# Column sums in 32-column tiles, and low parts made on Pool, in a gated attention-and-feed-forward block

## The chip, the cores and the metric

The kernel runs on one core of a Trainium2 chip. The metric is the device time of one execution in microseconds. Before the change it is 604.24 us, the median of three runs (603.97 to 604.48).

## What is computed

For each of two sequences of 1,024 rows of x (2,048 columns, f32) and a context of 2,048 x 2,048 the reference computes

```python
def fake_quant(x, scale, zp):
    q = clip(round(x / s + z), 0, 255)
    return (q - z) * s
x = x + tanh(g_xattn[0]) * (fake_quant(layernorm(x)) @ fake_quant(ctx))
x = x + tanh(g_ffn[0]) * (layernorm(x) @ (U * S @ V.T).T)      # rank 512
```

## The kernel before

The 2,048 rows are 16 tiles of 128 (NT = 16, eight to a context, TB = 8). Three stages follow each other for each tile on TensorE: `s1(t)` multiplies the quantised, transposed x by the quantised context (4 column quarters of 512, 16 matmuls each, 64 in all); `mm3(u)` multiplies the second normalised x, split into an f16 high and low part, by V, split likewise into v_hl (per half g of 8 k-tiles: 16 matmuls with V's high part, then 8 with its low part); `mm4(u)` multiplies that result by U (12 matmuls for each quarter). TensorE's list stands in full at L670 to L745.

Quantised values are held centred (q minus a rounded zero point, in bf16). What the fraction of the zero point takes away is added back as a correction: a row sum (`bvec`, from ScalarE's accumulator) and a column sum of the context (`corr`, L850). The column sums of the first context are matmuls by a 128 x 128 matrix of ones, one per k-tile (L516, 64 in all). Those of the second context already go in 32-column tiles (L520): four k-tiles each write 32 partitions of the bank, and two further f16 matmuls add the four groups up (L529, L530).

The first context is loaded in 32 chunks of 2 k-tiles x 512 columns (512 KB each), block n of 8 chunks being quarter n of the columns. For each chunk one engine makes u8 of f32 (ScalarE L756; Pool for chunks 1 to 5; DVE L1127 for the chunks of WHOLE, 27 and 31), and Pool (L252, even chunks) or DVE (L1131, odd ones) makes bf16. TensorE takes each chunk at once: two column sums, then two matmuls for each of tiles 0, 1 and 2 (in block 3 for tile 0 alone; tiles 1 and 2 follow whole, then tile 3's `s1`). Tiles 0 to 2 are transposed by TensorE, tile 3 by a DMA (L330).

For each tile and quarter Pool adds the row correction (L258, once a tile) and `corr` (L263) to x in `ring`, and DVE adds the product from PSUM (L1137) and takes its statistics (L1139): `x1_unit(t, n)`. When tile u has all four, DVE and ScalarE work out scale and bias. ScalarE writes x's high part (L811), DVE normalises into `xn` (L1174) and subtracts (L1177, `x_lo_half`), and SP issues the transposing DMA (L339). V arrives in 8 pieces of 2 k-tiles, is squared for a norm by ScalarE (L859), summed by TensorE (L668, `norm_sums`), scaled on ScalarE into its high part (L877) and on DVE into its low part (L1246, `v_low`, one instruction per piece). U's high and low parts (L884, L1252) follow `norm(1)`, which waits for `norm_sums(1)`.

Every engine's order is written out by hand: SP at L402 to L483 (all loads, stores and transposes in one queue), TensorE at L670, ScalarE at L887, DVE at L1255, Pool at L274. Each engine works its list in order and waits on semaphores of the others. Stages hold 10 chunks, so the load of chunk c waits until chunk c - 10 has been read. The pairs of loops at L693 and L1270 set the order in which chunks and tiles alternate.

## Time and profile before

| | |
|---|---|
| median of 3 runs | 604.24 us (603.97 to 604.48) |
| profiled execution | 604.71 us, span from first to last instruction 602.9 us |
| TensorE matmuls busy | 582.7 us (97%) |
| DVE, ScalarE, Pool busy | 381.7 us (63%), 212.4 us (35%), 191.4 us (32%) |
| granted TensorE clock | 1.00 over the whole span |
| moved by DMA | 102.21 MB, 387 GB/s in slices 2 to 4 of 40 (15 to 60 us) |

The duration of one matmul in the timeline includes its latency (0.38 us for 512 columns), so the start of the next is what tells its cost. Times of the timeline are from the span's first instruction. A row with xN joins N instructions in sequence, and a bracket at its end tells how long the engine stood before it and who released it.

### The profile page before, as it was taken

The numbers are of one execution on the slowest core, as the hardware profiler recorded it, in microseconds if no ns is written. First come the engines' busy times: TensorE is split into PE (matmuls) and PEld (weight loads), VectorE is DVE, ScalarE is ACT, GpSimd is POOL, SyncE is SP. The second block draws the span as 40 slices with busy tenths as digits, with TensorE's granted clock in tenths as the row PEclk, the third lists the DMA queues.
The fourth block names the chain that finished last, engine by engine and source line by source line (L and its number), as shares of the span: only waits on it lengthen the run. The fifth ranks groups of instructions, "written<-read, shape, count | busy, mean of one in ns | idle before, by whom it ended". The sixth has DMA issues, their size and how long they took to land.

```text
span 602.9 us, 7571 instructions
## 1 busy us (share of the span) xinstructions
PE 582.7 (97%) x2816; PEld 266.4 (44%) x2816; DVE 381.7 (63%) x703; ACT 212.4 (35%) x258; POOL 191.4 (32%) x149
## 2 busy tenths in 40 slices
PE   1899999999999999999999999999999999999998
PEld 1344444444444444445444444444444444444444
DVE  6939989995288962845375975647365665735212
ACT  5798978822041432456623310303011030301000
POOL 2899650002223419726505800220404030030000
DMA  8999985639828795998835344370906345181512
GB/s 280 387 387 387 309 240 128 116 122 196 239 55 240 186 216 189 241 304 268 241 123 150 81 84 54 66 190 12 223 35 147 116 90 172 30 163 20 138 53 104
DMA packets 143828, 102.21 MB, mean 170 GB/s; under 512 B 106672, under 2 KB 106928, under 8 KB 143792
## 3 DMA queue, kind: packets, MB, share of 16 engines
q1 hardware_dynamic: 134800, 84.43, 53.1%
q10 hardware_dynamic: 8992, 17.30, 9.2%
q8 instruction: 22, 0.36, 0.2%
q14 instruction: 14, 0.11, 0.1%
HBM read 58.99 MB, written 16.78 MB: 126 GB/s over the span
## 4 chain that ended last, share of the span: by engine, by line
PE 75%; DMA 11%; DVE 8%; issue 3%; SPq 2%; ACT 1%; POOL 1%; DVEq 0%; ACTq 0%
PE bank L553 23%; PE bank L584 16%; PE bank L651 8%; PE bank L650 8%; PE bank L655 8%; PE bank L589 8%; DMA v_hl<-in_ctx_dram 8%; DMA xT<-xs 4%; DVE v_hl L1246 1%; DVE xn L1174 1%; DVE xs L1177 1%; DVE ring L1137 1%; SPq L311 1%; PE bank L520 1%; POOL u8r L243 1%
## 5 line engine op out<-in xcount | busy, mean ns | idle before, releaser
L553 PE MATMUL bank<-q,qT 128*128 128x512 bf16 x896 | 201.5, 380 | 0.3 <-DVE ring L1137 0.3
L553 PEld LDWEIGHTS bank<-q,qT 128*128 128x128 bf16 x896 | 87.7, 98 | 107.1 <-issue 1.5
L258 POOL TENSOR_SCALAR ring<-ring,bvec 128x2048 f32<-128x2048 f32 x16 | 32.8, 2050 | 269.7 <-DVE bvec L1119 269.7
L584 PE MATMUL bank<-v_hl,xT 128*128 128x512 f16 x512 | 115.8, 379 | 0.9 <-DMA xT<-xs 0.9
L263 POOL TENSOR_TENSOR ring<-ring,corr 128x512 f32<-128x512 f32 x64 | 87.0, 1390 | 23.2 <-ACT corr L850 22.1
L651 PE MATMUL bank<-u_hl,hbuf 128*128 128x512 f16 x240 | 91.1, 380 | 0.0
L650 PE MATMUL bank<-u_hl,hbuf 128*128 128x512 f16 x240 | 91.0, 379 | 0.0
L1137 DVE SCALAR_TENSOR_TENSOR ring<-bank,const,ring 128x512 f32<-128x512 f32 x64 | 47.6, 743 | 58.2 <-PE bank L553 55.9
L1210 DVE SCALAR_TENSOR_TENSOR ring<-bank,cy,ring 128x512 f32<-128x512 f32 x63 | 46.4, 747 | 52.8 <-PE bank L655 52.8
L252 POOL TENSOR_SCALAR q<-u8r,const 128x1024 bf16<-128x1024 uint8 x52 | 63.9, 1236 | 45.4 <-ACT u8r L756 41.7
L584 PEld LDWEIGHTS bank<-v_hl,xT 128*128 128x128 f16 x512 | 49.8, 98 | 61.2 <-DMA xT<-xs 1.9
L797 ACT ACTIVATE ln<-ln,const 128x1 f32<-128x1 f32 x16 | 4.7, 294 | 189.8 <-DVE ln L1150 189.8
L655 PE MATMUL bank<-u_hl,hbuf 128*128 128x512 f16 x240 | 61.6, 379 | 0.0
L589 PE MATMUL bank<-v_hl,xT 128*128 128x512 f16 x256 | 60.6, 379 | 0.0
L1177 DVE TENSOR_TENSOR xs<-xn,xs 128x1024 f16<-128x1024 f32 x32 | 46.8, 1461 | 9.7 <-ACT xs L811 8.8
L1078 DVE BATCH_NORM_STATS2 st<-ring 128x6 f32<-128x512 f32 x64 | 40.3, 680 | 10.3 <-DMA ring<-in_x_dram 10.2
L1139 DVE BATCH_NORM_STATS2 st<-ring 128x6 f32<-128x512 f32 x64 | 44.5, 695 | 2.2
L811 ACT ACTIVATE xs<-ring,ln 128x1024 f16<-128x1024 f32 x32 | 38.2, 1233 | 20.4 <-DVE ln L1162 14.8
L589 PEld LDWEIGHTS bank<-v_hl,xT 128*128 128x128 f16 x256 | 25.0, 98 | 30.4 <-DVE v_hl L1246 0.4
L650 PEld LDWEIGHTS bank<-u_hl,hbuf 128*128 128x128 f16 x240 | 23.5, 98 | 28.5 <-issue 0.4
L655 PEld LDWEIGHTS bank<-u_hl,hbuf 128*128 128x128 f16 x240 | 23.5, 98 | 28.3
L1193 DVE SCALAR_TENSOR_TENSOR hbuf<-bank,hbuf 128x512 f16<-128x512 f32 x16 | 11.0, 687 | 39.4 <-ACT hbuf L825 39.4
(136 smaller groups left out, 493.3 us busy)
## 6 DMA issues: line engine op xcount, KB each, us to landing
out_dram<-ring SPq DMA_DIRECT2D x63, 256.0 KB, 3.5
ring<-in_x_dram SPq DMA_DIRECT2D x62, 256.0 KB, 3.9
v_hl<-in_ctx_dram SPq DMA_DIRECT2D x26, 512.0 KB, 11.5
stage<-in_ctx_dram ACTq DMA_DIRECT2D x17, 512.0 KB, 5.8
u_hl<-in_L_ffn_V_dram SPq DMA_DIRECT2D x8, 512.0 KB, 11.5
corr<-in_ctx_dram ACTq DMA_DIRECT2D x8, 512.0 KB, 6.7
stage<-in_ctx_dram SPq DMA_DIRECT2D x6, 512.0 KB, 11.5
q<-in_ctx_dram ACTq DMA_DIRECT2D x4, 512.0 KB, 8.8
```

The lines of the kernel that those rows point to most:

```text
L252: nc.gpsimd.tensor_scalar(q2_chunk(c), u8r[:, c % NU8, :], C_NC2, 1.0, ALU.add, ALU.mult)\
L263: nc.gpsimd.tensor_tensor(xq(t, n), xq(t, n), corr[:, n * W:(n + 1) * W], ALU.add).then_inc(x1_pre, 1)
L553: mm = nc.tensor.matmul(unit_bank(t, n)[:, :], qT_of(t)[:, k, :], q2[:, n, k, :], start=(k == 0), stop=(k == KT - 1))
L584: nc.tensor.matmul(h_bank(u)[:, :], xT[:, g, half, k % 8, :], v_hl[:, k, 0, :], start=(g == 0 and a == 0 and half == 0), stop=False)
L589: mm = nc.tensor.matmul(h_bank(u)[:, :], xT[:, g, 0, k % 8, :], v_hl[:, k, 1, :], start=False, stop=(g == 1 and a == 7))
L650: nc.tensor.matmul(y_bank(i)[:, :], t_hi[:, r, :], u_hl[:, n, r, 0, :], start=(r == 0), stop=False)
L651: nc.tensor.matmul(y_bank(i)[:, :], t_lo[:, r, :], u_hl[:, n, r, 0, :], start=False, stop=False)
L655: mm = nc.tensor.matmul(y_bank(i)[:, :], t_hi[:, r, :], u_hl[:, n, r, 1, :], start=False, stop=(r == RT - 1))
L1137: stt(xq(t, n), unit_bank(t, n)[:, :], C_A, xq(t, n), ALU.mult, ALU.add).then_inc(x1_ready, 1)
L1139: nc.vector.bn_stats(st2[:, t % R, n, :], xq(t, n)).then_inc(st2_ready, 1)
L1177: tt(xs[:, g, 1, :], xn[:, :], xs[:, g, 0, :], ALU.subtract).then_inc(xs_lo, 1)
L1210: stt(xq(u, n), y_bank(i)[:, :], cy[:, n:n + 1], xq(u, n), ALU.mult, ALU.add).then_inc(y_ready, 1)
```

## The change

- The first context's column sums go in the 32-column tiles of L520, in groups of two chunks (`colsum_pair`, behind every odd chunk). ScalarE copies the bank, divided by 32, to `corr` (`first_parts`), and one f32 matmul with ones adds the groups up (`first_total`). `column_correction(0, n)` waits for that.
- In block 3 TensorE takes tiles 0 and 1 (N3 = 2).
- WHOLE gains chunks 15, 19 and 23 (u8 made on DVE, not on ScalarE).
- SP loads all chunks first, then V's eight pieces (before, four of them alternated with the last four chunks).
- Tile 3's statistics, scale and u8 come one block sooner on DVE; ScalarE's and Pool's parts of it likewise (`op2(3)`, `pre_row(3)`).
- Pool makes V's low parts 3, 5 and 7, in two instructions each, and the normalised x of tiles 1, 2 and 3 (six halves). DVE still subtracts for x.
- `norm_sums(0)` moves into tile 3's `s1`, `norm_sums(1)` into mm3(1), behind its first high part.
- The lists of ScalarE and DVE are rewritten.

```diff
+    V_POOL = (3, 5, 7)
+    XN_POOL = (1, 2, 3)
+    N3 = 2
-        WHOLE = (27, 31)
+        WHOLE = (15, 19, 23, 27, 31)
...
+            def v_low(i):                                  # Pool
+                k = slice(2 * VORD[i], 2 * VORD[i] + 2)
+                pool.wait_ge(split_hi, i + 1)
+                nc.gpsimd.tensor_scalar(v_raw[:, k, :], v_raw[:, k, :], wsc[:, 3, 0:1], 1.0, ALU.mult, ALU.mult)\
+                    .then_inc(v_scaled, 1)
+                pool.wait_ge(v_scaled, V_POOL.index(i) + 1)
+                nc.gpsimd.tensor_tensor(v_hl[:, k, 1, :], v_raw[:, k, :], v_hl[:, k, 0, :], ALU.subtract)\
+                    .then_inc(v_lo_pool, 1)
+            def normalised_x(u, g):
+                pool.wait_ge(ln2_ready, u + 1)
+                pool.wait_ge(xs_lo, 2 * u + g)
+                nc.gpsimd.tensor_scalar(xn[:, :], xhalf(u, g), mean, scale, ALU.subtract, ALU.mult).then_inc(xn_pool, 1)
...
+            pre_row(G)
             for t in range(G):
                 pre(t, NQ - 1)
...
+                    if t == G:
+                        v_low(3)
+                        v_low(5)
+                        normalised_x(1, 0)
+                        v_low(7)
+                        normalised_x(1, 1)
+                        for u in XN_POOL[1:]:
+                            for g in range(2):
+                                normalised_x(u, g)
...
-            for c in range(12, CB - 4):
+            for c in range(12, CB):                        # SP
                 load_chunk(c)
-            for i in range(4):
-                load_v(VORD[i])
-                load_chunk(CB - 4 + i)
-            for i in range(4, CQ):
+            for i in range(CQ):
                 load_v(VORD[i])
...
+            def first_total(n):                            # TensorE
+                pe.wait_ge(parts_ready, n + 1)
+                nc.tensor.matmul(colsum_bank(0, n)[:, :], ones_f[:, :], corr[:, n * W:(n + 1) * W],
+                                 start=True, stop=True).then_inc(colsum_summed, 1)
+            def colsum_pair(n, i):
+                colsum(0, n, CK * (i - 1), CK * i + CK)
...
             for n in range(1, NQ):
                 for i in range(CQ):
-                    colsum(0, n, CK * i, CK * i + CK)
-                    for t in range(G if n < NQ - 1 else 1):
+                    need_chunk(CQ * n + i)
+                    if i % 2 == 1:
+                        colsum_pair(n, i)
+                    for t in range(G if n < NQ - 1 else N3):
                         s1_part(t, n, CK * i, CK * i + CK)
-            s1_part(1, NQ - 1)
-            s1_part(2, NQ - 1, 0, 12)
+                    if i == 1:
+                        first_total(n - 1)
+            for t in range(N3, G - 1):
+                s1_part(t, NQ - 1)
+            s1_part(2, NQ - 1, 0, 4)
+            first_total(NQ - 1)
+            s1_part(2, NQ - 1, 4)
+            s1_part(G, 0, 0, 8)
             norm_sums(0)
-            s1_part(2, NQ - 1, 12)
-            s1(G)
+            s1_part(G, 0, 8)
+            for n in range(1, NQ):
+                s1_part(G, n)
             mm3(0)
-            norm_sums(1)
             mm3(1)
...
+            def first_parts(n):                            # ScalarE
+                act.wait_ge(colsum_done, n + 1)
+                nc.scalar.activation(corr[:, n * W:(n + 1) * W], colsum_bank(0, n)[:, :], ACT.Copy,
+                                     scale=1.0 / GW).then_inc(parts_ready, 1)
...
+            first_parts(2)
+            op1(30)
             v_square(VORD[0])
+            v_square(VORD[1])
             column_correction(0, 2)
-            for j in VORD[2:6]:
+            for j in VORD[2:5]:
                 v_square(j)
+            first_parts(3)
+            v_square(VORD[5])
+            v_square(VORD[6])
             column_correction(0, 3)
-            for j in VORD[6:8]:
-                v_square(j)
+            v_square(VORD[7])
...
                     op2(c)                                 # DVE
-                    if n == 1 and i == 0:
+                    if n == 0 and i == 0:
                         sums1(3)
-                    elif n == 1 and i == 1:
                         variance1(3)
-                    elif n == 1 and i == 2:
+                    elif n == 0 and i == 1:
                         quantise(3)
...
             norm(0)
+            x_lo_half(0, 0)
             x1_unit(1, NQ - 1)
             x1_unit(2, NQ - 1)
-            x_lo_half(0, 0)
+            x1_unit(3, 0)
             x_lo_half(0, 1)
-            x1_unit(3, 0)
             v_low(0)
             variance2(1)
             v_low(1)
             scale2(1)
-            for i in range(2, 4):
-                v_low(i)
+            v_low(2)
             x_lo_half(1, 0)
-            for i in range(4, VP):
-                v_low(i)
+            v_low(4)
+            v_low(6)
             x_lo_half(1, 1)
             variance2(2)
+            hid_lo(0)
             norm_sum_up(1)
             scale2(2)
             norm(1)
-            hid_lo(0)
             u_low(0)
             x_lo_half(2, 0)
+            u_low(1)
             x_lo_half(2, 1)
-            u_low(1)
```

## Rows read from the trace of the kernel before

**Rows 1.** The page: busy time of each engine.
```profile
PE 582.7 (97%) x2816; PEld 266.4 (44%) x2816; DVE 381.7 (63%) x703; ACT 212.4 (35%) x258; POOL 191.4 (32%) x149
```

**Rows 2.** Waits of TensorE: us in total, times, longest.
```profile
PE bank L516 <- POOL q L252: 13.6, 4, 11.3
```

**Rows 3.** Timeline of TensorE: start us, us, engine, line, instruction, count.
```profile
49.12 0.60 PE L516 MATMUL bank<-q,ones_b 128*128 128x512 bf16 x2
...
62.93 0.60 PE L516 MATMUL bank<-q,ones_b 128*128 128x512 bf16 x2
...
77.95 13.98 PE L553 MATMUL bank<-q,qT 128*128 128x512 bf16 x64
91.77 3.62 PE L584 MATMUL bank<-v_hl,xT 128*128 128x512 f16 x16
...
108.12 3.63 PE L584 MATMUL bank<-v_hl,xT 128*128 128x512 f16 x16 [0.41 <-DMA xT<-xs]
```

**Rows 4.** Timeline of TensorE around column sums of the second context.
```profile
320.65 1.03 PE L655 MATMUL bank<-u_hl,hbuf 128*128 128x512 f16 x4
321.61 1.05 PE L520 MATMUL bank<-q,ones_b 128*32 128x512 bf16 x16
322.59 0.39 PE L553 MATMUL bank<-q,qT 128*128 128x512 bf16 x1
```

**Rows 5.** L668: durations ns (min/median/max) of f32; the page's group of bf16 loads.
```profile
L668 PEld LDWEIGHTS bank<-ssq,ones_f x4: 190/190/191, 76.7 to 102.2; 128*128 128x128 f32 x4
...
L553 PEld LDWEIGHTS bank<-q,qT 128*128 128x128 bf16 x896 | 87.7, 98 | 107.1 <-issue 1.5
```

**Rows 6.** Timeline of DVE and of Pool, 43 to 52 us.
```profile
44.56 0.75 DVE L1137 SCALAR_TENSOR_TENSOR ring<-bank,const,ring 128x512 f32<-128x512 f32 x1 [2.24 <-POOL ring L263]
...
48.71 1.02 DVE L1131 TENSOR_SCALAR q<-u8r,const 128x1024 bf16<-128x1024 uint8 x1
...
46.97 4.83 POOL L252 TENSOR_SCALAR q<-u8r,const 128x1024 bf16<-128x1024 uint8 x4
```

**Rows 7.** The page: DMA issues, KB each, median us to landing.
```profile
v_hl<-in_ctx_dram SPq DMA_DIRECT2D x26, 512.0 KB, 11.5
```

**Rows 8.** Timeline of ScalarE and DVE at the end of block 3.
```profile
70.17 1.06 ACT L859 ACTIVATE hbuf<-u_hl 128x1024 bf16<-128x1024 f32 x1
...
71.22 0.76 ACT L850 ACTIVATE corr<-bank,const 128x512 f32<-128x512 f32 x1
...
74.05 0.73 DVE L1137 SCALAR_TENSOR_TENSOR ring<-bank,const,ring 128x512 f32<-128x512 f32 x1
...
79.49 0.75 DVE L1137 SCALAR_TENSOR_TENSOR ring<-bank,const,ring 128x512 f32<-128x512 f32 x1
```

**Rows 9.** Timeline of Pool and DVE, 78 to 90 us.
```profile
78.83 5.42 POOL L263 TENSOR_TENSOR ring<-ring,corr 128x512 f32<-128x512 f32 x4
...
83.15 2.18 DVE L1177 TENSOR_TENSOR xs<-xn,xs 128x1024 f16<-128x1024 f32 x1
...
88.75 1.27 DVE L1246 SCALAR_TENSOR_TENSOR v_hl<-u_hl,wsc,v_hl 128x1024 f16<-128x1024 f32 x1
```

**Rows 10.** Lines over the whole span: ns min/median/max, first and last start.
```profile
L1174 DVE TENSOR_SCALAR xn<-ring,ln x32: 803/811/1640, 82.3 to 554.0; 128x1024 f32<-128x1024 f32 x32
L1177 DVE TENSOR_TENSOR xs<-xn,xs x32: 1224/1226/2873, 83.2 to 554.9; 128x1024 f16<-128x1024 f32 x32
L1137 DVE SCALAR_TENSOR_TENSOR ring<-bank,const,ring x64: 730/745/753, 44.6 to 548.2; 128x512 f32<-128x512 f32 x64
L263 POOL TENSOR_TENSOR ring<-ring,corr x64: 1259/1268/2249, 43.3 to 532.1; 128x512 f32<-128x512 f32 x64
L258 POOL TENSOR_SCALAR ring<-ring,bvec x16: 1965/1972/2399, 32.4 to 526.4; 128x2048 f32<-128x2048 f32 x16
```

**Rows 11.** Timeline of TensorE and ScalarE around the second sum of norms.
```profile
102.22 0.29 PE L668 MATMUL bank<-ssq,ones_f 128*128 128x8 f32 x2
...
114.18 2.54 ACT L884 ACTIVATE u_hl<-stage,us_scale 128x512 f16<-128x512 f32 x4
```

143 lines of the change are left out of this document (83 added, 60 removed).

## The prediction

> **What bounds it now.** The page comes first: TensorE is busy 582.7 of 602.9 us [rows 1], so the end of this kernel is set by how much TensorE has to do and by how long it stands still. The view of waits, TensorE only, says where it stands still: 13.6 us behind Pool's `q`, 11.3 of them before its first matmul [rows 2]. In mm3(1), at 108.12, it stands 0.41 [rows 3]. Behind that there is hardly a wait that could take anything back, so what this change shifts in the first 125 us stays in the total; the only thing that it touches later is x of tile 3. Third comes TensorE's timeline. In the first context's blocks 1 and 2 a chunk takes two column sums and six products; block 2 starts at 49.12 and block 3 at 62.93, 13.8 us later. Tile 3's 64 matmuls take 77.95 to 91.77, which gives the slot: 13.82 / 64 = 0.216 us. mm3(0) starts at 91.77 and reads V's first low part 16 slots later, at 95.22 [rows 3]. Last come the timelines of the engines that feed it, below.
>
> **Column sums.** 64 matmuls go: 64 x 0.216 = 13.8 us. They come back as 16 groups of four 32-column tiles, each between ordinary matmuls. The second context shows that form: four ordinary matmuls start at 320.65 and would hand over at 321.51, the tiles start at 321.61 (+0.10), and sixteen of them, four slots or 0.86, last until 322.59 (+0.12) [rows 4]. A lone group so costs 0.216 + 0.10 + 0.12 = 0.43 us; sixteen 6.9 us. Then four f32 totals of 512 columns. No f32 matmul of that width is in the trace. The small one of the norms is recorded as two passes (two calls, four records), and its weights load in 190 ns where bf16 ones take 98 [rows 5]. Bounds: two passes at full rate, 0.43 us; each pass twice as long, as its weights are, 0.86. I take 0.86, because the one f32 duration that I can compare is doubled: 3.5 us (1.7 at the other end). TensorE's own work falls by 13.8 - 6.9 - 3.5 = 3.4 us.
>
> The two gaps of 0.10 and 0.12 decide how much of that there is. The Trainium skill (TensorEngine Tiling (Array Packing), Theoretical Speedup) gives up to 4x for a dimension of 32; by that alone a group would cost one slot and the saving be 3.4 us larger. The same page (Key Properties) says that a change of tiling mode drains the engine, which speaks against small groups; the rows agree, 0.22 us a visit.
>
> **How much arrives at the end of block 3.** In block 0 only the columns behind chunk 5 count, the rest waits for chunks and transposes: 3 x 0.43 become 2 x 0.43, 0.43 earlier. Blocks 1 and 2 each trade 16 slots (3.45) for 4 x 0.43 + 0.86 = 2.58: 0.87 earlier each. But chunk 16 is made by Pool from 46.97 on at 1.2 us apiece (ready 48.2), and its list up to there is unchanged; TensorE would be there at 49.12 - 0.43 - 0.87 = 47.8 and waits about 0.4. Chunk 17 is worse. DVE made it from 48.71, behind three units of tile 0 to 2, and had 2.24 us of idle time ahead of those [rows 6]. Into that idle time go tile 3's statistics, its scaling and all of chunk 15; they overfill it by about 1.5 us, chunk 17 comes at 51.2 and two waits, 0.9 for it and 0.5 for the bank of tile 2, follow. Block 3 starts at 47.8 + 1.8 + (13.8 - 0.87) = 62.6, against 62.93. ScalarE loses three chunks and the DMA order puts V behind the chunks, which brings the last chunk 5 us sooner, so block 3 doesn't wait (before: 0.7). Two chunk loads now wait for DVE in SP's queue; a load takes 11.5 us from issue to landing [rows 7], so a few microseconds of lateness behind them are hidden by that queue; without it they would delay every chunk behind. Block 3, now with two tiles: 8 x 4 x 0.216 + 4 x 0.43 + 0.86 = 9.5, to 72.1. Then 0.86 + 0.86 + 12 x 0.216: tile 3 starts at 76.4, against 77.95. **1.5 us are gained here.**
>
> **What is late next.** The last correction of columns (L850) stood in `corr` at 71.98 (71.22 + 0.76) [rows 8]. Now the sums are ready at about 71.4, `first_parts(3)` takes 0.7, and ScalarE's list puts two squares of V (1.24 apiece: 1.06 and the read of the accumulator) ahead of the correction: 71.4 + 0.7 + 2.5 + 0.8 = 75.4. Pool's addition (1.27) is its next step, so tile 0's last unit starts at 76.8, not 74.05. Everything that mm3(0) needs hangs on that unit: the scale of x, then x's low parts, then V's low parts on DVE. TensorE reaches mm3(0) at 76.4 + 13.8 + 0.14 + 0.4 (tile 3's bank) = 90.8 and wants the first low part of V 3.45 later, at 94.2, 1.0 earlier than before.
>
> DVE from 76.8: 4.3 us to the scale and norm (before: 5.4 with 1.2 of waiting) is 81.1; first half of x 3.1 (as before, with 0.95 behind Pool) 84.2; three units of 1.38, 88.3; second half 2.0 alone, 90.4; the first V part 1.3 alone, 91.7. Alone, it would be in time, and so would the two behind it.
>
> **But it isn't alone.** Pool used to be idle from 84.25 (78.83 + 5.42) on. The subtraction for x that ran beside it took 2.18 us; V's first low part ran alone in 1.27 [rows 9]; the shortest for x is 1.224, and x's normalisation goes from 0.803 to 1.640, while the unit that reads PSUM is 0.730 to 0.753 in all 64 [rows 10]. So a DVE instruction with two SBUF operands, or a fast one, stands until Pool's is through. Pool now gets, in exactly this stretch, three products of V (half of 1.97 us: 1.0) and three subtractions of 1,024 columns (two of 1.27: 2.5), and four normalisations of 1.0. Whatever DVE starts behind a subtraction stands up to 2.5 us. Second half of x: +2.6 (one subtraction, part of a product). V's part 0: +2.1. It is there at 96.0 to 96.3, so TensorE waits 1.7. Behind it DVE delivers every 1.6 and 2.1 us (its variance and scale of tile 1 stand between), TensorE uses one in 0.43: 1.2 and 1.7 more. In the second half of mm3(0) the parts 4 and 6 are late by 1.7 and 0.9, behind Pool's last subtraction. Sum 7.2.
>
> Whether V's low parts on DVE are held is the disputed size: they never met Pool before. Bounds: nothing (as the units reading PSUM, 0.745) and the whole of Pool's instruction (as x's subtraction, 1.224 to 2.873). I take the latter; both read two SBUF operands. Without it the sum loses 4.5. The Trainium skill (SBUF — State Buffer, Summary: rules for kernel authors) says the same of any DVE instruction with two SBUF inputs, "the second one to issue **fully blocks** until the first finishes"; for this instruction no row shows it.
>
> mm4(0): the product of norms moves from the start of mm3(1) to 16 slots into it. Before, ScalarE ended the high parts of U's third quarter at 114.18 + 2.54 = 116.7, 14.4 behind that product (102.22 + 0.14) [rows 11]; 1.4 of it was DVE still at tile 1's x. Leaves 13.0; the quarter is wanted 56 slots behind the product, 12.1: 0.9 of waiting. Some 0.3 more for U's low parts from the late DVE: 1.2 together.
>
> **Sum.** Against the profiled execution (span 602.9, 604.71 in all, 0.47 above the median of 604.24): -1.0 (mm3(0) at 90.8, not 91.77) - 0.4 (the wait of mm3(1), which falls inside the new ones) + 7.2 + 1.2 = +7.0. From the median: **611 us**.
>
> **Rivals.**
> *The saving arrives* (faster). DVE and Pool hardly hold each other here: then V's parts come at 91.7, 93.3 and 95.4 and mm3(0) doesn't wait. -1.0 - 0.4 + 0.9 (U's high parts, in every case) + 0.3 (x of tile 1, just late) = -0.2; with totals at 0.43 each some 0.9 off, and if a lone group cost only its slot, as inside the run of sixteen, some 1.2 more: 604.24 - 2.3 = 601.9. For it: the units at 0.745 beside a busy Pool. Against: 1.64 and 2.87. It decides at about 1.5 us of standing before V's third part. Chance 0.27.
> *Half of it.* Only x's instructions are held, V's aren't: +7.0 - 4.5 = +2.5, 606.7. Chance 0.20.
> *A wash.* Blocking and saving cancel, or Pool's parts fall between DVE's: within 1.2 us, 604.2. Chance 0.12.
> *Pool itself late.* Should an f32 total cost 1.7 or Pool's subtraction of mixed types take longer than 2.5, 613 and more. Chance 0.06.
> *Forecast* 611 us, its own range 608 to 612.5: 0.35.
>
> A measurement of this kernel tells 0.2%, 1.2 us, from no change. Faster 0.27, same 0.12, slower 0.20 + 0.06 + 0.35 = 0.61. Range 601.5 to 612.5: from the faster rival's end, a little under it, to the forecast with its unknowns; outside stay the last rival and what would be faster still.
>
> **What would show it.** Right: on DVE the subtractions for x and V's low parts (before L1177 and L1246) above 2 us beside Pool between 87 and 106; TensorE waiting for `v_hl` of DVE, 5 us or more; tile 3 starting near 76.4; groups 0.43 apart from their neighbours; corr's last row ending near 75.4. Wrong: V's low parts on DVE at 1.27 as before (then 606.7 or less), mm3(0) started near 89 with no wait behind it (faster), or f32 totals at 0.43.

## The result, and the profile of the changed kernel

The changed kernel takes **622.43 us** (median of four runs, 621.98 to 622.91); the kernel before, run beside it, 604.36 (603.97 to 604.87). The ratio is 1.030 (95% interval 1.0286 to 1.0312): slower by 18.1 us, where 611 was forecast and 601.5 to 612.5 given as the range. The sign was right, the size was not. The profiled execution took 621.98 us, its span is 620.2.

The page of the changed kernel, its row of engines (it answers to [rows 1]) and its row of the granted clock, one digit for each fortieth of the span (15.5 us):

```profile
PE 584.5 (94%) x2795; PEld 263.4 (42%) x2824; DVE 387.5 (62%) x697; ACT 210.9 (34%) x259; POOL 232.1 (37%) x161
...
PEclk9999999789999999999999999999999999999999
```

Two things are to be seen. Pool is 41 us busier than before; at the prediction's prices its twelve new instructions make 16.5 (3 x 1.0 for products, 3 x 2.5 for subtractions, 6 x 1.0 for normalisations). The six normalisations alone make 27.2 (L281 of the page). And TensorE's granted clock isn't whole any more: in the eighth and ninth slice, 109 to 140 us, it is below full, while it was 1.00 over the whole span of the kernel before. TensorE has less work and is busy longer (584.5 us against 582.7).

The view of waits, TensorE (us in total, times, longest), against [rows 2]:

```profile
PE bank L524 <- ACT qn L832: 13.5, 2, 13.3
PE bank L633 <- DVE v_hl L1320: 7.1, 4, 4.4
PE bank L547 <- DVE q L1202: 1.7, 3, 0.9
PE bank L699 <- DVE u_hl L1326: 1.6, 4, 0.8
PE bank L588 <- DMA qT<-qn: 1.5, 1, 1.5
...
PE bank L694 <- ACT u_hl L946: 0.6, 1, 0.6
```

The first row is the start of the kernel, as before. The second is the one that was forecast: V's low parts. Where it stands shows TensorE's timeline, which answers to [rows 3]:

```profile
77.79 1.89 PE L588 MATMUL bank<-q,qT 128*128 128x512 bf16 x8
...
89.43 3.63 PE L588 MATMUL bank<-q,qT 128*128 128x512 bf16 x16 [0.98 <-DVE ring L1208]
92.89 3.62 PE L622 MATMUL bank<-v_hl,xT 128*128 128x512 f16 x16
96.67 0.61 PE L633 MATMUL bank<-v_hl,xT 128*128 128x512 f16 x2 [0.17 <-DVE v_hl L1320]
98.29 0.60 PE L633 MATMUL bank<-v_hl,xT 128*128 128x512 f16 x2 [1.01 <-DVE v_hl L1320]
100.42 1.04 PE L633 MATMUL bank<-v_hl,xT 128*128 128x512 f16 x4 [1.53 <-DVE v_hl L1320]
...
109.32 3.60 PE L633 MATMUL bank<-v_hl,xT 128*128 128x512 f16 x8 [4.41 <-DVE v_hl L1320]
112.71 4.77 PE L622 MATMUL bank<-v_hl,xT 128*128 128x512 f16 x16
...
119.74 3.63 PE L622 MATMUL bank<-v_hl,xT 128*128 128x512 f16 x16 [0.40 <-DMA xT<-xs]
124.93 0.38 PE L694 MATMUL bank<-u_hl,hbuf 128*128 128x512 f16 x1
```

Tile 3 starts at 77.79 and not at 76.4: the gain of 1.5 us is 0.2. mm3(0) starts at 92.89 (before: 91.77). mm4(0) starts at 124.93; in the kernel before it started at 113.3, so 11.6 of the 17.3 us by which the span grew are there already. The row at 109.32 has another thing: its eight matmuls take 3.4 us until the next row starts, 0.43 each, twice the slot. The granted clock by stretches of 2 us (its length, the busy us and counts of PE, PEld, DVE, ACT and POOL, then the clock, the DMA share and GB/s) says why:

```profile
106.00:108.00 2.00, 0.00 (x0) 0.00 (x0) 2.00 (x2) 1.88 (x4) 2.00 (x1) 1.00 0.28 55
108.00:110.00 2.00, 0.68 (x2) 0.28 (x3) 2.00 (x2) 0.47 (x2) 2.00 (x2) 0.55 1.10 206
110.00:112.00 2.00, 2.00 (x6) 0.75 (x5) 0.47 (x1) 0.00 (x0) 2.00 (x1) 0.50 0.01 1
...
114.00:116.00 2.00, 2.00 (x8) 0.84 (x7) 1.62 (x4) 0.52 (x2) 0.00 (x0) 0.74 0.02 4
```

From the end of the 4.41 us of standing still the clock is at 0.5, the 1.2 GHz level, until 115. The same happens at 136 to 138 us, behind four waits for U's low parts (0.81 and three of 0.27).

Who is late? Timeline of DVE and of Pool in this stretch, against [rows 9]:

```profile
93.48 3.14 DVE L1320 SCALAR_TENSOR_TENSOR v_hl<-u_hl,wsc,v_hl 128x1024 f16<-128x1024 f32 x1
...
104.12 2.09 DVE L1251 TENSOR_TENSOR xs<-xn,xs 128x1024 f16<-128x1024 f32 x1 [3.75 <-POOL xn L281]
...
114.05 1.23 DVE L1251 TENSOR_TENSOR xs<-xn,xs 128x1024 f16<-128x1024 f32 x1 [3.58 <-issue]
...
99.29 4.74 POOL L281 TENSOR_SCALAR xn<-ring,ln 128x1024 f32<-128x1024 f32 x1 [3.75 <-DVE ln L1233]
...
108.18 5.78 POOL L281 TENSOR_SCALAR xn<-ring,ln 128x1024 f32<-128x1024 f32 x1
```

V's low part that the prediction called the disputed size takes 3.14 us beside Pool and 1.27 alone (L1320: 1.272 to 3.143 over five): it is held, as forecast. But what keeps DVE standing for 3.75 and 3.58 us is Pool's normalised x, L281, priced at 1.0 us. The profile names it for the first; the second it puts down to "issue", but DVE's subtraction waits for that tile, and Pool's instruction ends at 113.96, 0.09 before it starts. The six take 3.78 to 5.78 us. Three take 3.78; the 5.78 has two of V's low parts on DVE beside it (106.13 to 110.47), so what is above 3.78 goes with DVE's work. The same instruction on DVE is 0.8 us [rows 10].

### The profile page after: what moved, and what is told of

The parts are those of the page before. It is cut to its first block, busy times and chain, and to the rows that moved or that the text cites. A ratio compares the mean times of both kernels' runs of the same rounds, so it can differ in the third digit from the quotient of the medians.

```text
span 620.2 us, 7587 instructions
## 1 busy us (share of the span) xinstructions
PE 584.5 (94%) x2795; PEld 263.4 (42%) x2824; DVE 387.5 (62%) x697; ACT 210.9 (34%) x259; POOL 232.1 (37%) x161
## 4 chain that ended last, share of the span: by engine, by line
PE 70%; DVE 12%; POOL 5%; DMA 4%; issue 4%; SPq 2%; ACT 2%; ACTq 0%; DVEq 0%; POOLq 0%
PE bank L588 25%; PE bank L622 14%; PE bank L633 7%; PE bank L694 7%; PE bank L695 7%; PE bank L699 7%; POOL xn L281 3%; DVE ring L1208 2%; DMA out_dram<-ring 2%; DMA v_hl<-in_ctx_dram 2%; DVE xs L1251 1%; PE bank L547 1%; DVE xn L1248 1%; SPq L345 1%; DVE qn L1181 1%
## 5 line engine op out<-in xcount | busy, mean ns | idle before, releaser
L588 PE MATMUL bank<-q,qT 128*128 128x512 bf16 x868 | 198.5, 381 | 6.0 <-DMA qT<-qn 1.5
L588 PEld LDWEIGHTS bank<-q,qT 128*128 128x128 bf16 x896 | 85.8, 98 | 112.0 <-issue 6.2
L622 PE MATMUL bank<-v_hl,xT 128*128 128x512 f16 x512 | 116.9, 382 | 0.4 <-DMA xT<-xs 0.4
L286 POOL TENSOR_TENSOR ring<-ring,corr 128x512 f32<-128x512 f32 x64 | 88.3, 1410 | 29.5 <-ACT corr L910 28.6
L633 PE MATMUL bank<-v_hl,xT 128*128 128x512 f16 x256 | 62.5, 387 | 7.1 <-DVE v_hl L1320 7.1
L1251 DVE TENSOR_TENSOR xs<-xn,xs 128x1024 f16<-128x1024 f32 x32 | 48.4, 1514 | 24.1 <-POOL xn L281 12.6
L281 POOL TENSOR_SCALAR xn<-ring,ln 128x1024 f32<-128x1024 f32 x6 | 27.2, 4527 | 28.1 <-DVE ln L1233 23.0
```

Of the source, the lines that this page charges most:

```text
L281: nc.gpsimd.tensor_scalar(xn[:, :], xhalf(u, g), mean, scale, ALU.subtract, ALU.mult).then_inc(xn_pool, 1)
L286: nc.gpsimd.tensor_tensor(xq(t, n), xq(t, n), corr[:, n * W:(n + 1) * W], ALU.add).then_inc(x1_pre, 1)
L588: mm = nc.tensor.matmul(unit_bank(t, n)[:, :], qT_of(t)[:, k, :], q2[:, n, k, :], start=(k == 0), stop=(k == KT - 1))
L622: nc.tensor.matmul(h_bank(u)[:, :], xT[:, g, half, k % 8, :], v_hl[:, k, 0, :], start=(g == 0 and a == 0 and half == 0), stop=False)
L633: mm = nc.tensor.matmul(h_bank(u)[:, :], xT[:, g, 0, k % 8, :], v_hl[:, k, 1, :], start=False, stop=(g == 1 and a == 7))
L1251: tt(xs[:, g, 1, :], xn[:, :], xs[:, g, 0, :], ALU.subtract).then_inc(xs_lo, 1)
```

## Experiments

Each ratio is to runs of the kernel before in the same batch; its median was 604.1 to 604.5 us in all of them. L numbers are those of the kernel in question.

### Pool's subtraction

In the first batch Pool's normalisation is written with the negated mean, which DVE computes anyway, so that it adds instead of subtracting:

```diff
-                mean, scale = ln2[:, u % 2, 0:1], ln2[:, u % 2, 8:9]
+                neg, scale = ln2[:, u % 2, 2:3], ln2[:, u % 2, 8:9]
-                nc.gpsimd.tensor_scalar(xn[:, :], xhalf(u, g), mean, scale, ALU.subtract, ALU.mult).then_inc(xn_pool, 1)
+                nc.gpsimd.tensor_scalar(xn[:, :], xhalf(u, g), neg, scale, ALU.add, ALU.mult).then_inc(xn_pool, 1)
```

> The changed kernel, with Pool's normalised x computed as (x + negated mean) x scale instead of (x - mean) x scale: the same operands, shape and scalars by pointer, only the first operation is an addition. Theory A (on Pool a tensor-scalar instruction that subtracts costs 3.8 us for 1,024 columns, one that adds costs 1.1 to 1.2 like the other tensor-scalar instructions of Pool): the six instructions fall from 3.8 us and more to about 1.2, the wait of 4.4 us in mm3(0) goes, and the kernel lands near 611 us. Theory B (two f32 scalars by pointer with an f32 result are what is slow): they stay at 3.8 and the kernel at 622.

**613.03 us**, ratio 1.0145 (1.0125 to 1.0165): 9.4 of the 18 us are one operation code. Line L281 of this kernel (ns min/median/max, first and last start), and its wait of TensorE for V's low parts:

```profile
L281 POOL TENSOR_SCALAR xn<-ring,ln x6: 1188/1670/3196, 99.0 to 141.0; 128x1024 f32<-128x1024 f32 x6
```
```profile
PE bank L633 <- DVE v_hl L1320: 4.7, 5, 1.8
```

1.19 us at the least against 3.78, the longest wait 1.8 instead of 4.4, and in the profiled execution the clock stays whole. This kernel has no wait for U's low parts nor for `qT` at 197 either: its profiled span is 10.2 us shorter (610.0), 5.6 of that ahead of mm4(0) (119.38 against 124.93). To have the operation by itself, nine forms were put ahead of Pool's work in the kernel before, on a scratch tile (`xn`), while DVE has little to do; `a` and `b` are columns of 128 scalars (each waits for the one before it; the semaphores are left out here):

```diff
+            nc.gpsimd.tensor_scalar(xn[:, :], xn[:, :], a, b, ALU.subtract, ALU.mult)
+            nc.gpsimd.tensor_scalar(xn[:, :], xn[:, :], a, b, ALU.add, ALU.mult)
+            nc.gpsimd.tensor_scalar(xn[:, :], xn[:, :], a, 1.0, ALU.subtract, ALU.mult)
+            nc.gpsimd.tensor_scalar(xn[:, :], xn[:, :], a, 1.0, ALU.add, ALU.mult)
+            nc.gpsimd.tensor_scalar(xn[:, :], xn[:, :], b, a, ALU.mult, ALU.subtract)
+            nc.gpsimd.tensor_scalar(xn[:, :], xn[:, :], b, a, ALU.mult, ALU.add)
+            nc.gpsimd.tensor_scalar(xn[:, :], xn[:, :], EPS, 1.0, ALU.subtract, ALU.mult)
+            nc.gpsimd.tensor_tensor(xn[:, 0:W], xn[:, 0:W], xn[:, W:HW], ALU.subtract)
+            nc.gpsimd.tensor_tensor(xn[:, 0:W], xn[:, 0:W], xn[:, W:HW], ALU.add)
```

> The kernel before, with nine operations of Pool on a scratch tile of 128x1024 f32 ahead of its work, to have their durations by themselves; the whole kernel's time is not what is looked at (it becomes some 10 us longer). Pool's own form is subtract then multiply with two columns of scalars: theory A expects 3.8 us for it, 1.2 us for add then multiply, 3.8 us for every form with a subtraction of a column and 1.2 us for every form with an addition. Rival B (the cost is of two scalars from memory and not of the subtraction): add then multiply with two columns takes as long as subtract then multiply, and both are shorter with the constant 1.0. The tensor_tensor forms on 512 columns take 1.25 us whichever the operation.

Pool's timeline of that kernel, in the order of the diff:

```profile
2.94 3.78 POOL L277 TENSOR_SCALAR xn<-xn,const,ones_f 128x1024 f32<-128x1024 f32 x1
6.83 1.19 POOL L279 TENSOR_SCALAR xn<-xn,const,ones_f 128x1024 f32<-128x1024 f32 x1
8.12 4.17 POOL L281 TENSOR_SCALAR xn<-xn,const 128x1024 f32<-128x1024 f32 x1
12.38 1.12 POOL L283 TENSOR_SCALAR xn<-xn,const 128x1024 f32<-128x1024 f32 x1
13.60 3.79 POOL L285 TENSOR_SCALAR xn<-xn,ones_f,const 128x1024 f32<-128x1024 f32 x1
17.50 1.19 POOL L287 TENSOR_SCALAR xn<-xn,ones_f,const 128x1024 f32<-128x1024 f32 x1
18.77 3.64 POOL L289 TENSOR_SCALAR xn<-xn 128x1024 f32<-128x1024 f32 x1
22.50 1.26 POOL L291 TENSOR_TENSOR xn<-xn 128x512 f32<-128x512 f32 x1
23.84 1.26 POOL L293 TENSOR_TENSOR xn<-xn 128x512 f32<-128x512 f32 x1
```

Every tensor_scalar with a subtraction takes 3.6 to 4.2 us, first or second operation, column or constant; every one with an addition 1.1 to 1.2. Where two tensors are combined the operation makes no difference. Theory A holds; the number of scalars (rival B) makes 0.07 us with an addition, and with a subtraction the form with one column is the longer one. The whole kernel took 618.4 us in its one run, which says nothing here.

### Which of Pool's new jobs

Three kernels give the jobs back to DVE: x, V's low parts, both (`XN_POOL = ()`, `V_POOL = ()`, their calls out of Pool's list and into DVE's); a fourth has V on DVE and x on Pool with the addition.

> The changed kernel, with the normalised x of tiles 1 to 3 back on DVE, V's low parts 3, 5 and 7 still on Pool. Theory A (Pool's normalised x is most of the loss): about 610 us, TensorE's waits in mm3(0) of V's low parts 5 us instead of 7, no fall of the granted clock. Rival (V's low parts on Pool, whose subtraction holds DVE, are most of the loss): 618 us or more.

> The changed kernel, with all eight low parts of V on DVE and x still normalised on Pool. Theory A: Pool's 3.8 us for a half of x stays on the path to x's low parts of tiles 1 and 2, so 617 to 619 us. Rival (V's low parts on Pool are most of the loss): 610 us or less.

> The changed kernel with both on DVE: only the column sums in 32-column tiles, tile 3 a block sooner, and the rewritten lists are left. Both theories say that blocking by Pool accounts for nearly all: by the rows the last unit of tile 0 is 3 us later and V's low parts on DVE take 3.9 us more than in the change, so 606 to 608 us. If it is 603 or less, the column sums bring what their slots promise; if it is over 612, the loss lies in the lists and not in Pool's work.

> V's low parts on DVE, x of tiles 1 to 3 normalised on Pool by the addition form (1.2 us a half). Theory A: Pool's x costs nothing once it takes 1.2 us, and gains nearly nothing, 608 to 610 us, against 619.4 with the subtracting form: 10 us for the one operation. Rival (Pool's x blocks DVE whatever its form): 613 or more.

| | x on Pool, subtracting | x on Pool, adding | x on DVE |
|---|---|---|---|
| V's parts 3, 5, 7 on Pool | 622.4 (the change) | 613.0 | 614.0 |
| V's parts all on DVE | 619.4 | 612.1 | **609.2** |

The intervals of the ratios are 1.0138 to 1.018 (614.0), 1.0212 to 1.0279 (619.4), 1.0094 to 1.0152 (612.1) and 1.0067 to 1.0097 (609.2). Read down and across: the subtraction costs 9.4 us with V on Pool and 7.4 without. Pool's work with the addition still costs 3.9 us against none of it. V alone costs 4.8 and x alone 2.9, which don't add up, and each kernel is slower than was expected of it. The clock is in these prices: in the profiled executions of three of the kernels (614.0, 619.4, 612.1) it fell, though that was not expected of the first; in those of 613.0 and 609.2 it didn't. TensorE's rows of the kernel with x on DVE and V on Pool:

```profile
102.06 1.89 PE L631 MATMUL bank<-v_hl,xT 128*128 128x512 f16 x4 [2.46 <-DVE v_hl L1318]
103.74 5.73 PE L620 MATMUL bank<-v_hl,xT 128*128 128x512 f16 x16
```

These twenty matmuls take 7.1 us and would take 4.3 at the full clock, and no wait behind them takes the 2.8 us in before mm4(0), at 121.53; the kernel with x on Pool, adding, is there at 119.38. The kernel with x on DVE took 612.7 and 613.0 us in the two executions whose mean clock was 0.997, and 615.0 and 615.1 in those at 0.994 and 0.992. So a part of the 4.8 is the clock and not Pool; how much of each price is, no run shows.

With none of Pool's new work TensorE waits 1.6 us for V's low parts (7.1 in the changed kernel), but the kernel is still 5 us over the kernel before. What is left of the change is the tile sums and the lists; the last two groups take them apart.

### Does the fall of the clock cost anything?

The stall of 4.41 us is filled with work that nobody needs:

```diff
                 if u == 1 and g == 0:
                     norm_sums(1)
+                if u == 0 and g == 1:
+                    pe.wait_ge(corr_ready, NQ)
+                    for f in range(18):
+                        nc.tensor.matmul(bank[7][:, :], xT[:, g, 0, f % 8, :], v_hl[:, KORD[g][f % 8], 0, :],
+                                         start=True, stop=True)
```

> The changed kernel, with 18 matmuls (their results go to a bank that nobody reads) in TensorE's list ahead of the first low part of V in the second half of mm3(0), where it stood still for 4.41 us at 109.32 and then ran 24 matmuls at half the clock. By full-clock slots of 0.216 us they take 3.9 us, so they fit into the stall. Theory A (the fall of the granted clock is paid for by the standstill, and the 2.9 us between 109 and 116 are lost beside the wait): the wait falls to 0.5 us, the granted clock stays at 1.0 from 100 to 120, mm4(0) starts 2.5 to 3 us sooner than at 124.93, and the time is 618.5 to 620.5, though this kernel computes more. Rival B (the clock falls for another reason, or mm4(0) waits for U's parts anyway): the clock still falls, or the start of mm4(0) does not move, and the time is 622 to 623. Rival C (the matmuls read what VectorE and Pool write and hold them up): over 624.

**623.67 us**, ratio 1.0318 (1.0294 to 1.0342): not faster. TensorE's timeline and the granted clock of this kernel:

```profile
106.19 4.05 PE L629 MATMUL bank<-v_hl,xT 128*128 128x512 f16 x18
110.07 1.89 PE L638 MATMUL bank<-v_hl,xT 128*128 128x512 f16 x8
...
119.67 5.31 PE L622 MATMUL bank<-v_hl,xT 128*128 128x512 f16 x16 [2.39 <-DMA xT<-xs]
```
```profile
100.00:102.00 2.00, 1.60 (x4) 0.58 (x5) 0.34 (x1) 1.97 (x4) 2.00 (x1) 0.50 0.96 312
102.00:104.00 2.00, 2.00 (x7) 0.77 (x6) 0.00 (x0) 2.00 (x4) 2.00 (x2) 0.65 0.39 152
```

The stall went, the eight matmuls at 110.07 run at full rate, the first half of mm3(1) ends 2 us sooner than in the changed kernel, and then TensorE stands 2.39 us for tile 1's second half of x until 119.67, where it came at 119.74 in the changed kernel. That half hangs on Pool's 5.78 us at 108.18, on DVE's subtraction at 114.05 and the DMA behind it. So in the changed kernel the fall of the clock behind 109 cost next to nothing by itself: the time it took lay inside a later wait (there 0.40 us of it were left, at 119.74), and theory A falls on this point. That doesn't hold for every kernel: in the one with x on DVE, above, no later wait took it in. The clock doesn't follow the waits alone either. In this kernel it fell at 100 to 104, behind waits of 0.17, 1.01 and 1.53 us; in the profiled executions of the changed kernel and of the one with the addition the same three waits (they agree to 0.01) were followed by the full clock. And it fell once more behind the 2.39 us, where sixteen matmuls took 5.31 us instead of 3.63; mm4(0) starts at 126.55. This profiled execution is the slowest of the four, 626.07 us at a mean clock of 0.986; the others took 621.7 to 623.7 at 0.992 to 0.996, where the changed kernel took 622.0 to 622.9 at 0.991 to 0.994.

### The column sums alone

The kernel before with the 32-column tiles, `first_parts` and `first_total`, with ScalarE's list adapted to them, and nothing else of the change:

> The kernel before with the column sums alone: groups of four 32-column tiles behind every odd chunk and an f32 total per block, everything else in its old place (block 3 with one tile, tile 3 late, chunks 15, 19 and 23 on ScalarE, V's low parts and x on DVE). By the slots 3.4 us of TensorE's work go. Theory C (the trade of slots is sound but DVE's low parts of V, which had 1.6 us of slack at the most, become the bound): mm3(0) starts 1 to 2 us sooner, waits of about 1 us appear behind V's low parts, 603 to 604.5 us. Rival (the tiles themselves lose, by their switches and by corr coming later): 605 or more. If all of it arrived: 601.

**606.38 us**, 1.0036 (1.0019 to 1.0052): 2.1 us slower with 3.4 us less work by the forecast's slots, as the rival to theory C has it. TensorE's waits showed one of 2.44 us for a chunk of block 3, so the next two take tile 1 into the loop over block 3's chunks, the second with V's loads moved too:

```diff
-                    for t in range(G if n < NQ - 1 else 1):
+                    for t in range(G if n < NQ - 1 else 2):
...
-            s1_part(1, NQ - 1, 0, 4)
+            s1_part(2, NQ - 1, 0, 4)
             first_total(NQ - 1)
-            s1_part(1, NQ - 1, 4)
-            s1_part(2, NQ - 1, 0, 12)
+            s1_part(2, NQ - 1, 4, 12)
```

> The kernel before with the column sums in 32-column tiles, as in the run of that part alone (606.38), and tile 1's last block taken into the loop over the chunks beside tile 0's, so that TensorE has twice the work for each chunk of the last block. Theory D (what the tiles save was given back as waits for the last chunks, 2.44 us at one of them): that wait falls to under 0.8 us, mm3(0) starts at 91.5 to 92.5 instead of 93.98, and the time is 604 to 605. Rival E (the chunks are late for every order, since their transfers set the pace): the waits move and their sum stays at 6 us, and the time is 606 or more.

> The kernel of the run with tile 1 in the loop, with V's loads behind all the chunks of the first context, as the change has them. Theory D: VectorE no longer waits 0.84 us for the last chunk's transfer, mm3(0) starts another 0.3 to 0.8 sooner, and the time is 603.3 to 604.7, at best 0.1% below the kernel before. Rival F (V's squares on ScalarE come later, and with them root2 and the high parts): the high parts of V or the norms are waited for, and the time is 605 to 607.

**606.53** (1.0022 to 1.0046) and **613.36 us** (1.0131 to 1.0158). The wait for the chunk fell to 0.23 as theory D has it, and nothing was won: mm3(0) started at 93.95 instead of 93.98. D falls, and E with it: the time is what E gave, but the chunks are no longer waited for. In the second kernel the loss is larger than D or F had it: V's loads came later while ScalarE's squares of V kept their place in its list, so ScalarE stood for a load, and DVE behind it. Rows of ScalarE and of DVE:

```profile
63.30 1.06 ACT L874 ACTIVATE hbuf<-u_hl 128x1024 bf16<-128x1024 f32 x1 [7.31 <-DMA u_hl<-in_L_ffn_V_dram]
```
```profile
67.60 0.21 DVE L1138 TENSOR_SCALAR bvec<-r1p,const 128x1 f32<-128x1 f32 x1 [5.02 <-ACT qn L793]
```

A load that is moved in one queue must be moved in the list of whoever waits for it. The next pair is about the last correction: block 3 goes back to the full-width sums, blocks 0 to 2 keep the tiles; the first has tile 1 behind the loop, the second in it.

```diff
+                    if b == 0 and n == NQ - 1:
+                        mm = nc.tensor.matmul(colsum_bank(b, n)[:, :], ones_b[:, :], q2[:, n, k, :],
+                                              start=(k == 0), stop=(k == KT - 1))
+                    else:
...
-            first_parts(3)
             v_square(VORD[5])
             column_correction(0, 3)
```

> The kernel before with the column sums in 32-column tiles for blocks 0 to 2 only; block 3 keeps the full-width sums, so its correction comes without the copy, the f32 product and the second copy. Theory G (what the tile sums cost by themselves, 2.1 us, is the last correction's longer way: 73.6 to 74.0 instead of 71.2, and tile 0's last product, the list behind it and mm3(0) late by the same): the last correction starts at 71.0 to 71.8, mm3(0) at 91.0 to 92.0, and the time is 603 to 604.6. Rival H (the tile sums cost where they run, by changes of mode, by totals between the chunks): mm3(0) stays at 93 or later and the time at 605.5 or more. Rival I (the chunks set the pace of the whole stage, so that nothing before the last of them can be won): the time is that of the kernel before within 0.1%.

> The same with tile 1's last block inside the loop over the chunks, so that TensorE's saving of 2.6 us in blocks 0 to 2 can be used while it waits for the last chunks. Theory G: mm3(0) at 90 to 91.5 and the time 602 to 604; rival I: the column sums of block 3 end later by tile 1's share (14 slots of 0.216 us, 3 us) and the last correction with them, at 73 or later, so that the time is 605 to 607.

**604.76** (ratio 1.0009, 1.0 to 1.0017) and **605.49 us** (1.0014 to 1.0032). The rows of the last correction on ScalarE, of tile 0's last product on DVE and of mm3(0), first with tiles in all blocks, then with the full width in block 3 (before: 71.22, 74.05 and 91.77 [rows 3, 8]):

```profile
73.59 0.78 ACT L869 ACTIVATE corr<-bank,const 128x512 f32<-128x512 f32 x1 [0.61 <-PE bank L524]
...
76.14 0.75 DVE L1160 SCALAR_TENSOR_TENSOR ring<-bank,const,ring 128x512 f32<-128x512 f32 x1 [1.16 <-PE bank L558]
...
90.52 3.63 PE L558 MATMUL bank<-q,qT 128*128 128x512 bf16 x16 [0.42 <-DVE ring L1160]
93.98 3.62 PE L589 MATMUL bank<-v_hl,xT 128*128 128x512 f16 x16
```
```profile
72.06 0.76 ACT L875 ACTIVATE corr<-bank,const 128x512 f32<-128x512 f32 x1
...
74.61 0.75 DVE L1164 SCALAR_TENSOR_TENSOR ring<-bank,const,ring 128x512 f32<-128x512 f32 x1
...
92.46 3.62 PE L593 MATMUL bank<-v_hl,xT 128*128 128x512 f16 x16
```

Two things can hold mm3(0), and the rows of all five kernels fit the later of them.

One is TensorE's own work behind the last chunk: 96 slots, 20.7 us, in the kernel before from 70.91 to 91.77 without a gap. The last chunk doesn't come sooner for anything that TensorE saves ahead of it: DVE starts on its bf16 at 68.35 in the kernel before, at 68.68 with tiles in three blocks and at 69.20 with tiles in four, and in these two it stood 1.08 and 0.84 us for the transfer. So the wait for the chunk grows, from 0.28 us to 1.09 and 2.44. That is rival I, and it takes the whole saving of blocks 0 to 2. In block 3 the f32 total, 0.86, comes on top.

The other is the chain from the last correction: tile 0's last product, DVE's list behind it, the bank that tile 3's last quarter needs, 3.5 us more. From product to mm3(0) it makes 17.4 to 17.8 us where that bank is waited for (76.52 to 93.95 and 75.25 to 92.70, both with tile 1 in the loop, and 76.14 to 93.98), and the kernel before, at 74.05, has 0.3 us to spare at the most. With tile 1 in the loop the chunks are no longer waited for, and the chain holds instead: 1.8 us for the bank in both.

Block 3's form is worth 1.4 of the 2.1 us, the size that theory G gave, but not by G's path alone. Of the 1.5 us by which mm3(0) comes sooner (93.98 to 92.46) 0.42 is the wait for the bank, at the end of G's chain; 0.86 is the total that TensorE no longer makes behind the last chunk, and 0.3 that it is through with that chunk's sums sooner (70.90 against 71.22). And the gain that G forecast (603 to 604.6, and 602 to 604 with tile 1 in the loop) doesn't come, because TensorE's work behind the chunk is next, or the chain. No kernel of this group beats the kernel before.

### The lists

Four kernels start from the one with both jobs back on DVE (609.16). Tile 3's statistics back in block 2; tile 1 out of the loop with the last correction one square sooner; then block 3 at full width with tile 1 out of the loop and in it; then the norm sums back in their places.

> The version with V's low parts and x on DVE (609.2 us), with tile 3's statistics, scale and u8 back in block 2 on DVE and ScalarE. Theory D: the waits for chunks 13, 15 and 17 (1.7 us) mostly go but TensorE waits later for the same DVE chain, 608 to 609 us. Rival (the early tile 3 is the loss): 606 or less.

> The version with V's low parts and x on DVE (609.2 us), with one tile in block 3 as before, the last f32 total inside tile 1's matmuls and the last column correction behind one square of V. Theory D (the rest of the loss is the last correction of columns, 4 us later than before since block 3 carries two tiles): it comes 3 us sooner, the wait of 0.97 for tile 3's bank and the 1.6 for V's low parts go, 606 to 607 us. Rival (the loss lies in blocks 1 and 2, where TensorE waits for chunks): 609.

> The changed kernel with V's low parts and the normalised x back on VectorE (609.16, mm3(0) at 92.91, tile 0's last product at 77.73), block 3's column sums at full width and its correction behind five squares, tile 1's last block behind the loop. It keeps of the change the tile sums of blocks 0 to 2, tile 3's earlier statistics and the order of the loads. Theory G: the last correction comes at 72 to 73.5 instead of 75.53, tile 0's last product at 74.5 to 76, mm3(0) at 90 to 91.8 (the span from that product to mm3(0) was 15.2 us with tile 3 early and 17.7 in the kernel before), V's low parts are still waited for by 1 to 2 us, and the time is 604 to 606. Rival J (VectorE's list for mm3(0) and mm4(0) is what counts, not its start): mm3(0) comes sooner and V's low parts are waited for longer by the same, so that mm4(0) stays at 115.4 or later and the time at 607 or more. A time under 603.5 would be a version that beats both.

> The same with tile 1's last block inside the loop over the chunks, as the change has it. Theory G: the last correction comes 1 to 2 us later than in the run beside it and the time is 0.5 to 2 us above that one's; rival I (the chunks set the pace): it is within 0.3 us of it or faster.

610.08 us (1.0078 to 1.0124), 608.11 (1.0039 to 1.0073), **608.36** (1.0054 to 1.0079) and 609.22 (1.007 to 1.0098). The first is over theory D's 608 to 609 and far from the rival, that the early tile 3 is the loss; the second lies between theory D (606 to 607) and its rival (609).

Tile 3 sooner is worth 1 us at most, and the intervals of the two kernels overlap. The chain from tile 0's last product to mm3(0) is shorter in the changed kernel, 15.2 us (77.71 to 92.89), but the product came 3.7 us later. The expectation of the third kernel puts the 15.2 down to tile 3's earlier statistics; the traces don't bear that out, for with tile 3 late the chain is 15.2 as well (78.83 to 94.00), and so it is with V and x back on DVE (77.73 to 92.91). What all three share is DVE's new order, where tile 3's first unit, which frees the bank, comes ahead of the second half of x (in the kernel before it comes behind).

In the third of the four the last correction came at 71.53 instead of 75.53, tile 0's last product at 75.14 instead of 77.73, and yet mm3(0) only at 92.62 instead of 92.91: now TensorE's 96 slots behind the last chunk hold it (71.76 to 92.62, no gap). mm4(0) starts at 115.63, and that with the time is rival J. DVE gives back most of what it won, standing for the sum of the norms, so that V's first low part comes at 91.05 (before: 88.75 [rows 9]):

```profile
80.72 0.17 DVE L1295 TENSOR_REDUCE wsc<-bank 128x1 f32<-128x8 f32 x1 [3.55 <-PE bank L711]
...
91.05 1.28 DVE L1318 SCALAR_TENSOR_TENSOR v_hl<-u_hl,wsc,v_hl 128x1024 f16<-128x1024 f32 x1
```

The fourth, with tile 1 in the loop, is 0.9 us over the third, as theory G has it.

The change moved `norm_sums(0)` into tile 3's products and `norm_sums(1)` into mm3(1). The last two kernels put the first back, then both:

```diff
-            s1_part(2, NQ - 1)
-            s1_part(G, 0, 0, 8)
+            s1_part(2, NQ - 1, 0, 12)
             norm_sums(0)
-            s1_part(G, 0, 8)
+            s1_part(2, NQ - 1, 12)
+            s1_part(G, 0)
...
             mm3(0)
+            norm_sums(1)
             mm3(1)
```

> The kernel of the run just before (608.36) with norm_sums(0) back in its place of the kernel before, inside tile 2's last block instead of inside tile 3's first. There VectorE stood 3.55 us for it at 80.72, and V's first low part came at 91.05 instead of 88.75. Theory K (the later norms are the rest of what the lists cost): V's first low part at 88.5 to 89.5, no wait for V's low parts (1.2 us now), mm4(0) at 114 to 114.6 instead of 115.63, and the time 606.5 to 607.3. Rival L (the norms are hidden, V's low parts are late by VectorE's order): the waits stay over 1 us and the time at 608 to 608.5.

> The same with norm_sums(1) back ahead of mm3(1) as well, where the change put it inside, 3.5 us later; it gates U's scales, cy and so the parts of U and every result of mm4(0). Theory K: the waits of 0.3 us in mm4(0) go, x(2) and what hangs on it come up to 3 us sooner, and the time is 605 to 606.5. Rival M (U's squares on ScalarE end at 104, so TensorE waits for them): the wait that it adds is under 0.5 us and the time that of the run beside it.

**606.98** (1.0024 to 1.0054) and **605.65 us** (1.0009 to 1.0041). The same two rows of the first of them:

```profile
77.88 0.17 DVE L1295 TENSOR_REDUCE wsc<-bank 128x1 f32<-128x8 f32 x1 [0.95 <-PE bank L711]
...
89.16 1.28 DVE L1318 SCALAR_TENSOR_TENSOR v_hl<-u_hl,wsc,v_hl 128x1024 f16<-128x1024 f32 x1
```

V's low parts are no longer waited for at all, and mm4(0) starts at 113.74 instead of 115.63: theory K. The medians differ by 1.4 us and the intervals of the ratios only touch, so the size is rougher than the mechanism. For the second sum the proof is weaker. The medians differ by 1.3 us, but the intervals overlap, and mm4(0) starts at the same time in both; only one wait of 0.3 us in mm4(0) is gone.

**The account**, by differences of medians from kernel to kernel: the subtraction 9.4 us, Pool's work at its right price 3.9, block 3's correction and tile 1's place 0.8 (the intervals overlap), the first sum of norms 1.4, the second 1.3 (not certain), and 1.2 to 1.5 left over against the kernel before for the tile sums of blocks 0 to 2, the loads and the order of the rest, which were not taken apart. The first two include what the clock's falls took. No kernel here is faster than the kernel before; the closest are 604.8 and 605.7.

## Why the prediction was right and wrong

**The step that failed** is a term of the sum: "four normalisations of 1.0", half of Pool's row of 1.97 us for 2,048 columns [rows 10]. They measured 3.78 to 5.78. That row (L258) adds and multiplies, the new instruction subtracts and multiplies, and every tensor_scalar of Pool in the kernel before adds and multiplies too: the nearest row differed in the one thing that counts. The price should have been marked as taken from another operation, with a bound above it; the rival "Pool itself late" had the mechanism, but on another of Pool's instructions and at 0.06. With the addition the same kernel takes 613.0, 0.5 over the upper bound, and its mm4(0) starts at 119.38, where the forecast's terms up to there (7.0 less the 1.2 inside mm4(0), on 113.3) give 119.1. That they agree so closely is owed in part to errors that cancel, as the next points show.

**Right.** A lone group of tiles is 0.43 us: in the changed kernel one starts at 36.58 and its successor at 36.91, behind a gap of 0.10. An f32 total costs 0.85 from 38.22 to 39.07, so the upper bound was the value; line L554 has two passes of 592 ns each and weights in 190. The waits for chunks 16 and 17 were 0.44 and 0.95, forecast 0.4 and 0.9. DVE's instructions with two SBUF operands are held by Pool: x's subtraction up to 2.88, V's low part 3.14 against 1.27. V's low part starts at 93.48 and ends at 96.62, 1.1 us behind the end of Pool's subtraction (92.57 to 95.54). The rule of the Trainium skill (SBUF — State Buffer, Summary: rules for kernel authors), that the second one to issue blocks fully until the first finishes, agrees with that. Pool's mixed subtraction, priced at 2.5, took 2.13 and twice 2.97. And V's low parts were waited for by 7.1 us where 7.2 was the sum, but the parts of it were 2.7 in the first half of mm3(0) and 4.4 in the second, against 4.6 and 2.6: two errors that cancelled.

**Wrong in the same direction, smaller.** The last correction started at 75.50 and ended at 76.26, forecast 75.4; tile 3 started 1.4 us later than forecast, because chunks 13 and 15 were waited for too (0.52 and 0.25) and the issue gaps of the groups add 0.8; the wait for tile 3's bank was 0.98, forecast 0.4. So mm3(0) started at 92.89 and not at 90.8. Rows of ScalarE and DVE at the end of block 3, against [rows 8]:

```profile
75.50 0.76 ACT L910 ACTIVATE corr<-bank,const 128x512 f32<-128x512 f32 x1
...
77.71 0.75 DVE L1208 SCALAR_TENSOR_TENSOR ring<-bank,const,ring 128x512 f32<-128x512 f32 x1 [4.01 <-POOL ring L286]
```

The prediction counted TensorE's saving as 1.0 us won at mm3(0) and gave the late correction no part in that. The runs show that mm3(0) waits for the later of two things, the last chunk with the work behind it and the chain from the last correction, and that neither got shorter by cheaper column sums in blocks 0 to 2. In the changed kernel it was the chain: 77.71 + 15.2 = 92.9.

**Not foreseen.** The move of `norm_sums(0)` was listed in the change and not priced; it holds V's scale and is worth about 1.4 us, by the difference of two medians. `norm_sums(1)` was priced, at 0.9. The fall of the clock was in no rival. And the end of the sum at mm4(0) was wrong: from there to the end the changed kernel loses another 5.7 us (17.3 less 11.6), where the one with the addition loses 1.0 (7.1 less 6.1): 2.2 in waits for U's parts behind Pool's x of tile 2 (5.30 us at 126.24), some at the lower clock from 136 to 138, 1.5 in one wait for `qT` at 197; the rest wasn't followed. The prediction named x of tile 3 as the only later thing touched, and gave it nothing.

## What to carry over

Before work goes to another engine, look for a row with the same operation, type and number of operands on that engine, and where there is none, time it alone or write it as one that has a row: here x - m became x + (-m), and 9.4 us came back. When an engine's work shrinks, find what that stage's end hangs on before the saving is counted: here the last chunk, the last correction with one product behind it, and a sum of norms. And when a load or a small product is moved in one list, follow everyone who waits for it in the others.

## What the runs showed of the hardware

- Pool's tensor_scalar on 128 x 1,024 f32 takes, by itself, 1.12 to 1.19 us with an addition and 3.64 to 4.17 with a subtraction, whichever operand; tensor_tensor of 512 columns takes 1.26 either way. The Trainium skill (GPSIMD Engine Reference, Engine selection) says that elementwise work with one input is roughly at line rate on this engine; that fits the addition (0.80 us is the shortest of the same shape on DVE) and not the subtraction.
- TensorE's granted clock fell to 0.5, the 1.2 GHz level, behind single stalls of 4.41 and 2.39 us and behind series such as 0.18, 1.45 and 2.46 (the run with x on DVE, 101 to 108 us). Behind 0.17, 1.01 and 1.53 it fell in one profiled execution and not in two others, and behind the 2.44 us of the kernel with the column sums alone not at all. The group of sixteen that ran into a fall took 4.77, 5.31 and 5.73 us instead of 3.62. Ahead of mm4(0) that cost next to nothing where a later wait took it in (the changed kernel) and up to 2.8 us where none did (x on DVE). The Trainium skill (TensorE: Matmul & The Clock Gate, Part 1) has the two levels, and that the count of slow matmuls varies from run to run of one kernel; the levels are those of the traces here, and the mean clock of one kernel's four executions went from 0.986 to 0.996.
- V's low part on DVE, an f32 scalar_tensor_tensor with two SBUF operands, is held until a tensor_tensor that Pool had started before it has ended: 3.14 us against 1.27, in the changed kernel, with Pool's instruction 0.91 us ahead of it. It goes the other way too: in the same kernel Pool's subtracting tensor_scalar takes 5.78 us beside two of V's low parts and 3.78 by itself.
